# Adjacency steps of one chunk of edges instead of two, with 24 x 131 source columns, in a graph attention and expert kernel

## The chip, the cores and the metric

The kernel runs on one core of a Trainium2 chip. The time is device time in microseconds of one execution. Three runs of the kernel before took 1892.36, 1878.16 and 1903.58 us; the median is 1892.36.

## The reference, cut to what matters

There are 3125 nodes with 256 features and 100000 edges, sorted by destination. A graph attention layer, then an expert layer; both add to x.

```python
x = _layernorm(x)
q, k, v = linear(x, wq, bq), linear(x, wk, bk), linear(x, wv, bv)
scores = jnp.sum(q[dst] * k[src], axis=-1) * scale          # one per edge
scores = scores + (edge_weight[:, None] @ we + be)[:, 0]
exp_s = jnp.exp(scores - segment_max(scores, dst)[dst])
attn = exp_s / jnp.maximum(segment_sum(exp_s, dst)[dst], 1e-12)
out = segment_sum(v[src] * attn[:, None], dst)
x1 = layer_norm(x + out + linear(x, ws, bs), g1, b1)
x2 = layer_norm(x1 + linear(gelu(linear(x1, w_ff1, b_ff1)), w_ff2, b_ff2), g2, b2)
# then for each node: expert = argmax of 32 router logits, out = relu(relu(xf @ W1[e] + b1[e]) @ W2[e] + b2[e])
```

## The kernel before, in words

The kernel turns the edge list into a dense matrix and does dense attention with it: adj[d, s] is the sum, over the edges from s to d, of exp of their edge term; an attention weight is adj[d, s] x exp(q.k).

**Ahead of the steps (0 to 157 us).** VectorE works on the edges, 98 rows of 1024 (8 chunks of 128 edges each): edge terms, guards by scans, a code for each edge (destination and block of its source), and the powers of the source's place in its block. It also counts which chunk each step reads: comparisons of a row of NS = 98 x PS entries (PS = 8/SUB, so NS = 392) with the step numbers, one for each of SBLK = 8 blocks of 128 slots (L990, L991), and 5 more for the windows (L1017, L1018). The edge table then goes to HBM, GpSimd gathers the chunks of each step with SBLK x SUB = 16 indirect DMAs (L598) and sets a row of ones by a memset (L602), VectorE makes the codes relative (L1026), TensorE transposes them into tables and ScalarE copies these. TensorE and ScalarE make k, q, v and x ws of the 25 node tiles beside that.

**The steps (157 to 888 us).** Destinations are cut into 625 windows of WIN = 5 nodes, edges into chunks of 128. One step handles SUB = 2 neighbouring chunks for one window: 1015 steps, in NG = 512 groups of GROUP = 2, so a group has GC = 4 chunks. `turns` unrolls BODY = 16 groups as one turn of a hardware loop; the first and the last turn are written out. For each chunk:

- TensorE, `distances` (L1356): a small bf16 product gives for each edge and each of LO = 128 columns the squared distance between the column and the source's place in its block, less one;
- ScalarE, `columns` (L784): relu with the scale -(edge term) turns it into Ys, the edge term in one column and zero elsewhere;
- VectorE, `one_hot` (L1055): Xs, a one-hot of the edge's code (window row x 25 blocks of 125 sources), two chunks in one operation of 128 x 250;
- TensorE, `product` (L1371): Xs (as weights) times Ys, summed over the step's two chunks in PSUM, two passes each (f32).

Then VectorE, `sums` (L1081), adds for each of the group's two steps the step before times keep (0 or 1) to the product, into `stage`, and SP stores `stage` to adj (L523). A sum reads the sum before it, so it waits for it: the group's second on sum_ord, the first on sums_ready. VectorE's order is sum, one_hot, sum, one_hot; the one-hots are for three groups ahead (STAGES = 4 buffers). In the loop each sum and each one-hot has a register instruction in front of it, which works out the place in the table.

TensorE's order per group g is: wait for Ys of g, distances of g + 2, wait for Xs of g, product of g. SP loads the powers every 8 groups, and stores zeros to xs_dram every 8.

**Attention (888 to 1487 us).** 25 tiles of 125 destinations: SP's and GpSimd's gather of the 125 last adj rows (L625), scores in SCH = 7 chunks of columns (L1392; 6 x 512 and 128; six matmuls each, four PSUM banks), `exclude` (L1104) and the maximum on VectorE (L1112), exp on ScalarE (L793), times adj on VectorE (L1122), transposes (L1411) and the product with V (L1404). TensorE runs scores of t + 1 ahead of the transposes of t. The first two tiles' gathers start in the middle of the steps.

**Behind it (1487 to 1886 us).** Feed-forward, router, and the 56 expert tiles.

## Time and profile before

| | |
|---|---|
| median of three runs | 1892.36 us |
| span of the profiled execution | 1885.6 us (the page gives no other time of it) |
| TensorE busy | 1656.9 us, 88% |
| VectorE busy | 1193.9 us, 63% |
| ScalarE busy | 965.5 us, 51% |
| one-hots, L1055 | 1024 x 412 ns |
| sums, L1081 | 1023 x 344 ns |
| relus, L784 | 2048 x 369 ns |
| granted clock of TensorE, mean | 0.917 |

A time such as 344 ns is from the start of an instruction until its last result is written. The next one on the same engine can start earlier, so group times are read from starts. The granted clock is 1.00 at 2.4 GHz and 0.50 at 1.2 GHz. Idle time of an engine counts only where it sets the end.

### The profile page before, as it was taken

Reading aid. Unit: us, or ns where it says so; the run is one execution under the profiler, and the core shown is the slowest. Engines: PE = TensorE matmul, PEld = TensorE weight load, DVE = VectorE, ACT = ScalarE, POOL = GpSimd, SP = SyncE. Lnnn points to the kernel's source line nnn. Section 1 sums busy time; section 2 is a strip of 40 time slices with the busy share of each in tenths; the row PEclk is TensorE's granted clock in tenths of the full one; section 3 lists DMA queues with packets and bytes.
Section 4 is the critical chain, followed back from the end, with each engine's and each line's share of the span. In section 5 each row is a group of like instructions: output and inputs, shape, how many; then the busy total and the mean of one; then the engine's idle time right before and its main releaser. Section 6 shows DMA issues by size and latency. Waiting matters only on the chain.

```text
span 1885.6 us, 41069 instructions
## 1 busy us (share of the span) xinstructions
PE 1656.9 (88%) x11015; PEld 1378.6 (73%) x11015; DVE 1193.9 (63%) x3327; ACT 965.5 (51%) x2962; POOL 300.8 (16%) x397
## 2 busy tenths in 40 slices
PE   2898999999799999999899999999999789419960
PEld 1796888888688888887688888888888779315640
DVE  3927898988688889898555555555555578701111
ACT  1566888888588888887233333333333345103210
POOL 0022000000000000000111111111110067375435
PEclk9999999999899999999999999999999889656555
DMA  6054333333433333334822222222210100047634
GB/s 159 28 129 115 104 105 104 106 103 105 140 104 104 106 105 103 104 105 112 164 76 77 76 76 76 76 78 75 76 75 37 53 17 0 6 117 214 181 113 121
DMA packets 226999, 180.40 MB, mean 96 GB/s; under 512 B 41884, under 2 KB 218038, under 8 KB 223544
## 3 DMA queue, kind: packets, MB, share of 16 engines
q1 hardware_dynamic: 189327, 112.46, 21.6%
q0 software_dynamic: 21408, 61.20, 9.7%
q10 hardware_dynamic: 16224, 6.27, 1.5%
q8 instruction: 17, 0.28, 0.1%
q14 instruction: 23, 0.19, 0.0%
HBM read 84.94 MB, written 99.11 MB: 98 GB/s over the span
## 4 chain that ended last, share of the span: by engine, by line
PE 78%; DVE 6%; DMA 5%; POOL 4%; issue 3%; SPq 2%; ACT 1%; POOLq 0%; DVEq 0%; ACTq 0%
PE bank L1371 29%; PE bank L1404 15%; PE bank L1392 11%; PE bank L1356 9%; PE bank L1411 3%; PE bank L1486 3%; PE bank L1493 2%; PE bank L1478 2%; PE bank L1444 2%; PE bank L1436 2%; POOL arena L691 2%; POOL xs_dram L669 2%; SPq L458 1%; DMA V<-in_x 1%; DMA arena<-in_x 1%
## 5 line engine op out<-in xcount | busy, mean ns | idle before, releaser
L784 ACT ACTIVATE arena<-bank,tables 128x128 f32<-128x128 f32 x2048 | 585.2, 369 | 144.5 <-PE bank L1356 144.4
L1371 PE MATMUL bank<-arena 128*125 128x128 f32 x4096 | 585.9, 286 | 11.8 <-DVE arena L1055 11.8
L1371 PEld LDWEIGHTS bank<-arena 128*125 128x125 f32 x4096 | 488.4, 188 | 65.1 <-DVE arena L1055 11.9
L1055 DVE TENSOR_TENSOR arena<-iota_row,tables 128x250 f32<-128x250 f32 x1024 | 421.1, 412 | 0.1
L1081 DVE SCALAR_TENSOR_TENSOR arena<-arena,tables,bank 125x128 f32<-125x128 f32 x1023 | 351.9, 344 | 86.5 <-PE bank L1371 37.1
L1404 PE MATMUL bank<-V,arena 125*125 125x256 f32 x1250 | 296.4, 382 | 5.6 <-ACT arena L810 5.6
L810 ACT COPY arena<-bank 125x500 f32<-125x500 f32 (+1 forms) x175 | 90.8, 533 | 379.5 <-PE bank L1411 379.5
L1404 PEld LDWEIGHTS bank<-V,arena 125*125 125x125 f32 x1250 | 223.3, 188 | 38.0 <-ACT arena L810 10.3
L1122 DVE CUSTOM_DVE_ANT_0 arena<-arena 125x3200 f32<-125x3200 f32 x25 | 87.3, 3493 | 222.2 <-ACT arena L793 222.2
L622 POOL COPY gidx<-arow 125x1 uint32 (+1 forms) x25 | 36.4, 1455 | 1182.2 <-DVE wk_sb L1122 856.7
L1356 PE MATMUL bank<-dist_rhs,arena 5*128 5x128 bf16 x2048 | 201.6, 218 | 4.2 <-DVE tables L1039 3.4
L1356 PEld LDWEIGHTS bank<-dist_rhs,arena 5*128 5x128 bf16 x2048 | 113.8, 93 | 66.3 <-issue 4.0
L1392 PE MATMUL bank<-k_hi,q_hi 128*125 128x512 f32 (+1 forms) x350 | 137.7, 393 | 10.3 <-DVE wk_sb L1112 6.9
L1392 PE MATMUL bank<-k_lo,q_hi 128*125 128x512 f32 (+1 forms) x350 | 133.2, 380 | 0.0
L1392 PE MATMUL bank<-k_hi,q_lo 128*125 128x512 f32 (+1 forms) x350 | 133.2, 380 | 0.0
L1112 DVE CUSTOM_DVE_ANT_0 arena<-bank,arena 125x512 f32<-125x512 f32 (+1 forms) x175 | 103.0, 631 | 28.0 <-PE bank L1392 19.1
L793 ACT ACTIVATE arena<-arena,wk_sb 125x512 f32<-125x512 f32 (+1 forms) x175 | 115.8, 679 | 9.6 <-DVE wk_sb L1117 9.6
L1271 DVE TENSOR_SCALAR arena<-bank 128x256 f32<-128x256 f32 x56 | 23.7, 424 | 152.7 <-PE bank L1493 152.7
L1411 PE MATMUL bank<-ident,arena 125*125 125x125 f32 x625 | 94.5, 276 | 2.7 <-issue 2.7
L1411 PEld LDWEIGHTS bank<-ident,arena 125*125 125x125 f32 x625 | 88.7, 190 | 9.4 <-issue 3.1
L1392 PEld LDWEIGHTS bank<-k_hi,q_hi 128*125 128x125 f32 x350 | 65.9, 188 | 30.5 <-DVE wk_sb L1112 13.2
L1478 PE MATMUL bank<-ident,V 128*128 128x128 f32 x112 | 37.2, 434 | 55.1 <-DMA V<-xs_dram 55.1
(219 smaller groups left out, 1665.5 us busy)
## 6 DMA issues: line engine op xcount, KB each, us to landing
adj<-arena SPq DMA_DIRECT2D x512, 125.0 KB
xs_dram<-zeros SPq DMA_DIRECT2D x64, 112.0 KB, 3.2
V<-xs_dram SPq DMA_DIRECT2D x56, 128.0 KB, 2.3
ys_dram<-arena SPq DMA_DIRECT2D x56, 128.0 KB, 1.9
w_dram<-in_L_ffn_W SPq DMA_DIRECT2D x2, 2048.0 KB
V<-in_x SPq DMA_DIRECT2D x5, 625.0 KB
q_dram<-arena ACTq DMA_DIRECT2D x25, 125.0 KB, 2.3
wq_sb<-q_dram SPq DMA_DIRECT2D x25, 125.0 KB, 7.8
```

What stands on the lines that cost most here:

```text
L784: ins = nc.scalar.activation(Ys[:, q, k, :], bank[2 + s][:, k * LO:(k + 1) * LO], ACT.Relu, scale=nval_tab[:, bass.ds(i, 1)])
L793: ins = nc.scalar.activation(Z[0:TILE, s, c:c + n], Z[0:TILE, s, c:c + n], ACT.Exp, bias=nmax[:, s:s + 1])
L810: nc.scalar.copy(PT[0:TILE, s, j:j + n, :], bank[4 + g % 2][0:TILE, 0:n * TILE].rearrange("p (n d) -> p n d", n=n)).then_inc(pt_ready, 1)
L1055: ins = V_.tensor_tensor(Xs[:, s, cols, :], iota_row[:, 0:TILE].unsqueeze(1).to_broadcast([P, SUB, TILE]), code_tab[:, bass.ds(g * GC + k ...
L1081: ins = V_.scalar_tensor_tensor(stage[0:TILE, q, k, :], prev, keep_tab[0:TILE, bass.ds(g * GROUP + k, 1)], ps, ALU.mult, ALU.add)
L1112: V_.tensor_tensor_reduce(out=Z[0:TILE, s, c:c + n], in0=bank[b % 4][0:TILE, 0:n], in1=Z[0:TILE, s, c:c + n], scale=1.0, scalar=-BIG, op0= ...
L1122: V_.tensor_tensor_reduce(out=Z[0:TILE, s, :], in0=Z[0:TILE, s, :], in1=A_sb[0:TILE, s, :], scale=1.0, scalar=0.0, op0=ALU.mult, op1=ALU.a ...
L1356: ins = mm(bank[2 + s][:, k * LO:(k + 1) * LO], dist_rows[:, j // LOADG, c:c + CHUNK], dist_rhs[:, :], start=True, stop=True)
L1371: ins = mm(o, Xs[:, j % STAGES, k, :], Ys[:, j % STAGES, k, :], start=(k % SUB == 0), stop=(k % SUB == SUB - 1))
L1392: ins = mm(bank[b % 4][0:TILE, 0:n], q[:, s, k, :], v[:, k, j, :].rearrange("p j l -> p (j l)"), start=(i == 0), stop=(i == len(parts) - 1))
L1404: ins = mm(bank[6 + s][0:TILE, 0:D], PT[0:TILE, s, j, :], V[:, j, :], start=(j == 0), stop=(j == NT - 1))
L1411: ins = tr(bank[4 + g % 2][0:TILE, j * TILE:(j + 1) * TILE], Z[0:TILE, s, (j0 + j) * LO:(j0 + j) * LO + TILE], ident[0:TILE, 0:TILE])
```

## The change

SUB goes from 2 to 1: a step is one chunk. There are 1406 steps, NG = 704 groups with GC = 2 chunks each, 44 turns for 32, SBLK = 11, NS = 784. The sources are cut into HI = 24 blocks of LO = 131 (24 x 131 = 3144 columns), so a one-hot has WIN x HI = MW = 120 columns. One operation `one_hots` makes both one-hots of a group (128 x 240), after the group's two sums. Keys are kept without gaps as 3125 columns padded to NCOL = 7 x 448, and scores go in 7 chunks of 448. Zero stores have 84 rows for 112, and there are 88 for 64. TensorE's product has two added waits on sums_ready.

```diff
-SUB = 2
+SUB = 1
-LO = 128
-ROW = NT * LO
+HI, LO = 24, 131
+ROW = HI * LO
+MW = WIN * HI
+KB = 448
+NCOL = 7 * KB
-ZROWS = MT * P // (2 * TURNS)
+ZROWS = -(-MT * P // (2 * TURNS * 12)) * 12
-SCH = [(c, min(512, ROW - c)) for c in range(0, ROW, 512)]
+SCH = [(c, KB) for c in range(0, NCOL, KB)]
...
-            od(V_.tensor_copy(s_row, bank[0][:, 0:NS]))
+            od(V_.tensor_copy(s_row[:, 0:512], bank[0][:, 0:512]))
+            od(V_.tensor_copy(s_row[:, 512:NS], bank[1][:, 0:NS - 512]))
+            dve.sem_inc(s_copied, 1)
...
-            def one_hot(g, s, k):
-                cols = slice(k * SUB, (k + 1) * SUB)
-                ins = V_.tensor_tensor(Xs[:, s, cols, :], iota_row[:, 0:TILE].unsqueeze(1).to_broadcast([P, SUB, TILE]),
-                                       code_tab[:, bass.ds(g * GC + k * SUB, SUB)].unsqueeze(2).to_broadcast([P, SUB, TILE]),
-                                       ALU.is_equal)
-                if k == GROUP - 1:
-                    ins.then_inc(x_ready, 1)
+            def one_hots(g, s):
+                V_.tensor_tensor(Xs[:, s, :, :], iota_row[:, 0:MW].unsqueeze(1).to_broadcast([P, GC, MW]),
+                                 code_tab[:, bass.ds(g * GC, GC)].unsqueeze(2).to_broadcast([P, GC, MW]),
+                                 ALU.is_equal).then_inc(x_ready, 1)
...
-                        ins = V_.scalar_tensor_tensor(stage[0:TILE, q, k, :], prev,
-                                                      keep_tab[0:TILE, bass.ds(g * GROUP + k, 1)], ps, ALU.mult, ALU.add)
+                        ins = V_.scalar_tensor_tensor(stage[0:MW, q, k, :], prev,
+                                                      keep_tab[0:MW, bass.ds(g * GROUP + k, 1)], ps, ALU.mult, ALU.add)
                     ins.then_inc(sum_ord if k < GROUP - 1 else sums_ready, 1)
-                    if not (isinstance(i, int) and i == TURNS - 1 and j > BODY - STAGES):
-                        one_hot(g + STAGES - 1, (q - 1) % STAGES, k)
+                if not (isinstance(i, int) and i == TURNS - 1 and j > BODY - STAGES):
+                    one_hots(g + STAGES - 1, (q - 1) % STAGES)
...
             def spread():
...
+                mm(bank[0][:, 0:512], ones[0:PP, :], s_diag[:, 0:512], start=True, stop=True)
+                mm(bank[1][:, 0:NS - 512], ones[0:PP, :], s_diag[:, 512:NS], start=True, stop=True).then_inc(rows_bc, 1)
                 pe.wait_ge(diag_set, 2)
+                pe.wait_ge(s_copied, 1)
...
                 pe.wait_ge(x_ready, g + 1)
+                wait_from(pe, sums_ready, g - STAGES + 1)
+                wait_from(pe, sums_ready, g - STAGES + 1)
...
-                        ins = mm(bank[b % 4][0:TILE, 0:n], q[:, s, k, :], v[:, k, j, :].rearrange("p j l -> p (j l)"),
+                        ins = mm(bank[b % 4][0:TILE, 0:n], q[:, s, k, :], v[:, k, c:c + n],
```

The order on VectorE inside the loop of the steps, one group before. L1081 is the sum, L1055 the one-hot; ISA is the register instruction in front of each, and the square brackets say what it waits for.

```order
L1081 ISA [waits sums_ready,stored2,prod_done]
L1081 SCALAR_TENSOR_TENSOR arena<-arena,tables,bank 125x128
L1055 ISA
L1055 TENSOR_TENSOR arena<-iota_row,tables 128x250
L1081 ISA [waits sum_ord]
L1081 SCALAR_TENSOR_TENSOR arena<-arena,tables,bank 125x128
L1055 ISA
L1055 TENSOR_TENSOR arena<-iota_row,tables 128x250
```

And one group of the change, where the sum is L1084 and the one-hot L1061:

```order
L1084 ISA [waits sums_ready,stored2,prod_done]
L1084 SCALAR_TENSOR_TENSOR arena<-arena,tables,bank 120x131
L1084 ISA [waits sum_ord]
L1084 SCALAR_TENSOR_TENSOR arena<-arena,tables,bank 120x131
L1061 ISA
L1061 TENSOR_TENSOR arena<-iota_row,tables 128x240
```

The second sum has moved up to stand right behind the first, on which it waits by sum_ord, and one of the two one-hots is gone.

On TensorE, in the written-out turn, two groups before. L1356 are the distances, L1371 the products:

```order
L1356 MATMUL bank<-dist_rhs,arena 128x128 [waits y_ready]
L1356 MATMUL bank<-dist_rhs,arena 128x128 x3
L1371 MATMUL bank<-arena 125x128 [waits x_ready]
L1371 MATMUL bank<-arena 125x128 x3
L1356 MATMUL bank<-dist_rhs,arena 128x128 [waits y_ready]
```

and in the change, where they are L1361 and L1378:

```order
L1361 MATMUL bank<-dist_rhs,arena 128x131 [waits y_ready]
L1361 MATMUL bank<-dist_rhs,arena 128x131
L1378 MATMUL bank<-arena 120x131 [waits sums_ready,x_ready]
L1378 MATMUL bank<-arena 120x131
L1361 MATMUL bank<-dist_rhs,arena 128x131 [waits y_ready]
```

Each group has half the matmuls, and the first product also waits on sums_ready.

## Rows read from the trace of the kernel before

**Rows 1.** source line L1081, the sums on VectorE: durations, first and last start

```profile
L1081 DVE SCALAR_TENSOR_TENSOR arena<-arena,tables,bank x1023: 332/346/349, 162.1 to 887.7; 125x128 f32<-125x128 f32 x171
L1081 DVEq FUSED_REGOPS  x960: 65/70/90, 185.0 to 866.5; - x192
```

**Rows 2.** chain of waits, 510 to 520 us (start us, us, what)

```profile
514.88 0.33 PE bank L1356 x4
515.20 1.07 PE bank L1371 x8
```

**Rows 3.** windows A:B: length, busy (x) of PE PEld DVE ACT POOL, PEclk, DMA share, GB/s

```profile
157.00:163.50 6.50, 5.57 (x31) 4.72 (x32) 3.81 (x12) 4.36 (x16) 0.00 (x0) 0.50 0.01 3
210.00:478.00 268.00, 268.00 (x2311) 224.80 (x2309) 240.92 (x770) 219.75 (x770) 0.10 (x1) 1.00 0.37 104
478.00:501.00 23.00, 11.23 (x98) 9.36 (x96) 8.77 (x29) 10.15 (x36) 3.15 (x4) 0.79 0.55 183
```

**Rows 4.** timeline of VectorE: start us, us, instruction, count, [idle before <-releaser]

```profile
499.31 0.35 DVE L1081 SCALAR_TENSOR_TENSOR arena<-arena,tables,bank 125x128 f32<-125x128 f32 x1 [13.54 <-DMA adj<-arena]
...
511.63 0.34 DVE L1081 SCALAR_TENSOR_TENSOR arena<-arena,tables,bank 125x128 f32<-125x128 f32 x1
511.89 0.41 DVE L1055 TENSOR_TENSOR arena<-iota_row,tables 128x250 f32<-128x250 f32 x1
512.26 0.35 DVE L1081 SCALAR_TENSOR_TENSOR arena<-arena,tables,bank 125x128 f32<-125x128 f32 x1
```

**Rows 5.** timeline of VectorE in one attention tile

```profile
1036.29 0.16 DVE L1131 RECIPROCAL wk_sb<-wk_sb 125x1 f32<-125x1 f32 x1
1036.61 0.48 DVE L1133 SCALAR_TENSOR_TENSOR ws_sb<-bank,wk_sb,x 125x256 f32<-125x256 f32 x1
1037.12 0.48 DVE L1137 SCALAR_TENSOR_TENSOR ws_sb<-bv_row,wk_sb,ws_sb 125x256 f32<-125x256 f32 x1
...
1038.30 0.43 DVE L1139 BATCH_NORM_STATS2 wv_sb<-x  x1 [0.23 <-DVE x L1138]
```

**Rows 6.** page, DMA issues: KB each, median us from issue to landing

```profile
ys_dram<-arena SPq DMA_DIRECT2D x56, 128.0 KB, 1.9
```

**Rows 7.** source line L517, the zero stores

```profile
DMA to landing us min/median/max: 2.5/3.2/4.6
```

**Rows 8.** timeline of VectorE ahead of the steps

```profile
68.50 0.76 DVE L983 TENSOR_SCALAR arena<-arena 98x1024 f32<-98x1024 f32 x1
...
75.46 0.43 DVE L990 TENSOR_SCALAR arena<-arena,step_col 128x392 f32<-128x392 f32 x1
75.92 0.56 DVE L991 TENSOR_REDUCE cnt<-arena 128x1 f32<-128x392 f32 x1
```

**Rows 9.** timeline of GpSimd: the first gather, and the memset behind the last

```profile
125.43 1.16 POOL L598 DMA_INDIRECT arena<-edge_tab,cidx  x1 [107.24 <-DMA edge_tab<-arena]
...
145.49 6.91 POOL L602 MEMSET arena<- 2x8192 bf16 x1
```

**Rows 10.** timeline of TensorE's weight loads in the scores of one tile

```profile
1008.39 0.18 PEld L1392 LDWEIGHTS bank<-k_hi,q_hi 128*125 128x125 f32 x1 [0.24 <-DVE wk_sb L1112]
...
1011.05 0.18 PEld L1392 LDWEIGHTS bank<-k_hi,q_hi 128*125 128x125 f32 x1
1011.28 0.18 PEld L1392 LDWEIGHTS bank<-k_lo,q_hi 128*125 128x125 f32 x1
1011.39 0.19 PEld L1392 LDWEIGHTS bank<-k_hi,q_lo 128*125 128x125 f32 x1
```

**Rows 11.** instructions by form, 1003 to 1164 us, x count | busy us, mean ns

```profile
L793 ACT ACTIVATE arena<-arena,wk_sb 125x512 f32<-125x512 f32 x42 | 30.5, 727 | 0.0
...
L793 ACT ACTIVATE arena<-arena,wk_sb 125x128 f32<-125x128 f32 x7 | 2.7, 391 | 0.0
```

**Rows 12.** chain of waits, 159 to 165 us, at the half clock

```profile
159.54 2.00 PE bank L1371 x8
161.54 0.54 PE bank L1356 x4
```

More of the change, by code:

```diff
@@ L112, in gnn_moe @@
         ones = sb("ones", [P, P])
-        iota_row = sb("iota_row", [P, P])
+        iota_row = sb("iota_row", [P, LO])
         step_col = sb("step_col", [P, SBLK])
@@ L137, in gnn_moe @@
         row = {k: v[0] for k, v in rows.items()}
-        with nc.sbuf_tensor("kT", [P, KH, NT, LO], F32) as kT, nc.sbuf_tensor("tables", [P, KH * ROW], F32) as tables:
+        with nc.sbuf_tensor("kT", [P, KH, NCOL], F32) as kT, nc.sbuf_tensor("tables", [P, KH * NCOL], F32) as tables:
             pass
-        k_lo = sb("k_lo", [P, KH, NT, LO], F32R)
-        k_hi = sb("k_hi", [P, KH, NT, LO], F32R)
+        k_lo = sb("k_lo", [P, KH, NCOL], F32R)
+        k_hi = sb("k_hi", [P, KH, NCOL], F32R)
         q_hi, q_lo = sb("q_hi", [P, 2, KH, TILE], F32R), sb("q_lo", [P, 2, KH, TILE], F32R)
@@ L153, in gnn_moe @@
         x1 = sb("x1", [TILE, NT, D])
-        ARENA = 19050
+        ARENA = 19260
         arena = sb("arena", [P, ARENA])
@@ L176, in gnn_moe @@
         assert SBLK * SUB * TABW <= edges_only
-        cmp_o = view(4 * P)
-        s_row, o_row, iota_c = view(4 * P), view(4 * P), view(4 * P)
-        cmp_s, s_row, o_row, iota_c = (v[:, 0:NS] for v in (cmp_o, s_row, o_row, iota_c))
+        cmp_o = view(NS)
+        s_row, o_row, iota_c = view(NS), view(NS), view(NS)
+        cmp_s = cmp_o
         diag_flat = view(SBLK * P)
@@ L295, in gnn_moe @@
             "code_set", "idx_set", "rel_set", "tabT_done", "tab_set", "keep_set"))
-        gath_in = [sem(f"gath_in{b}") for b in range(SBLK)]
+        s_copied = sem("s_copied")
+        gath_in = [sem(f"gath_in{b}") for b in range(-(-SBLK // 2))]
+        gathered = [16 * min(2, SBLK - 2 * b) for b in range(-(-SBLK // 2))]
         last_set, last_stored, last_in, arow_set = (sem(n) for n in ("last_set", "last_stored", "last_in", "arow_set"))
@@ L329, in gnn_moe @@
         x_t = x.rearrange("(t p) d -> p t d", p=TILE)
-        xs_v, ys_v = (v.ap().rearrange("(j p) d -> p j d", p=P) for v in (xs_dram, ys_dram))
+        xs_v, ys_v = (v.ap()[0:MT * P, :].rearrange("(j p) d -> p j d", p=P) for v in (xs_dram, ys_dram))
         out_t = out.rearrange("(t p) d -> p t d", p=TILE)
@@ L523, in put @@
                 sp.dma_start(adj_v[:, bass.ds(g * GROUP, GROUP), :],
-                             stage[0:TILE, j % STAGES, :, :]).then_inc(stored[j % STAGES], 16)
+                             stage[0:MW, j % STAGES, :, :]).then_inc(stored[j % STAGES], 16)
             turns(sp, put)
@@ L581, in _ @@
                            allow_small_or_imprecise_dtypes=True).then_inc(consts_set, 1)
-            nc.gpsimd.memset(kT[:, :, :, TILE:LO], 0.0).then_inc(consts_set, 1)
+            nc.gpsimd.memset(kT[:, :, N:NCOL], 0.0).then_inc(consts_set, 1)
             nc.gpsimd.memset(minus_half[:, :], -0.5).then_inc(consts_set, 1)
@@ L758, in _ @@
                 act.wait_ge(tabT_done, b + 1)
-                ps = bank[6 + b % 2][:, :].rearrange("p (c u i) -> p c i u", c=2, u=SUB)
+                ps = bank[6 + b % 2][:, 0:2 * SUB * P].rearrange("p (c u i) -> p c i u", c=2, u=SUB)
                 def steps(tab):
@@ L799, in key_parts @@
                 c, n = SCH[b]
-                j = slice(c // LO, (c + n) // LO)
-                nc.scalar.copy(k_hi[:, :, j, :], kT[:, :, j, :]).then_inc(k_hi_set, 1)
+                nc.scalar.copy(k_hi[:, :, c:c + n], kT[:, :, c:c + n]).then_inc(k_hi_set, 1)
             def weights(t, s, t_next, u):
@@ L1121, in weigh @@
                 dve.wait_ge(e_ready, t + 1)
-                V_.tensor_tensor_reduce(out=Z[0:TILE, s, :], in0=Z[0:TILE, s, :], in1=A_sb[0:TILE, s, :], scale=1.0,
+                V_.tensor_tensor_reduce(out=Z[0:TILE, s, :], in0=Z[0:TILE, s, :], in1=A_sb[0:TILE, s, 0:NCOL], scale=1.0,
                                         scalar=0.0, op0=ALU.mult, op1=ALU.add, accum_out=den[:, s:s + 1]).then_inc(p_ready, 1)
@@ L1317, in spread @@
                 pe.wait_ge(diag_set, 1)
-                mm(bank[0][:, 0:NS], ones[0:PP, :], s_diag, start=True, stop=True).then_inc(rows_bc, 1)
+                mm(bank[0][:, 0:512], ones[0:PP, :], s_diag[:, 0:512], start=True, stop=True)
+                mm(bank[1][:, 0:NS - 512], ones[0:PP, :], s_diag[:, 512:NS], start=True, stop=True).then_inc(rows_bc, 1)
                 pe.wait_ge(diag_set, 2)
+                pe.wait_ge(s_copied, 1)
                 mm(bank[1][:, 0:4 * PP], ones[0:PP, :], e_diag, start=True, stop=True).then_inc(rows_bc, 1)
```

63 lines of the change are left out of this document (31 added, 32 removed).

## The prediction

> **What bounds the kernel now.** The page's list of groups puts most of the time into the adjacency steps, so I read these lines first. Their sums on VectorE run from 162.1 to 887.7 us [rows 1]: 725.6 us. In the chain of waits a group of this stage is four distance matmuls (L1356, 0.33) and eight product passes (L1371, 1.07), nothing else [rows 2]: 1.40 us, or 1.39 by the starts. The windows show TensorE busy without a gap at a granted clock of 1.00 [rows 3]. Check: 512 groups x 1.39 = 712, and one stall of 13.54 us on an adj store [rows 4] makes 725.5. That is the stage.
>
> The timeline of VectorE shows how near the next bound is. Where its product was there in time, the starts are sum, +0.26 one-hot, +0.37 next sum [rows 4], at most 0.63 for such a pair, so 1.26 of the 1.39 us. A sum lasts 0.35 us, yet an independent successor starts 0.26 after it: they overlap.
>
> **TensorE's side of the change.** Two distances and four product passes are left per group: half of 1.39, 0.70 us (131 columns for 128 add 2%, 120 loaded columns for 125 take as much off). ScalarE's relus take 219.75/770 = 0.29 us each [rows 3], 0.6 a group. Both fall under VectorE, so TensorE leaves the bound.
>
> **VectorE's side.** A group was sum, one-hot, sum, one-hot; each sum waits for the sum before it, and a one-hot lay between. Now it is sum, sum, one-hot: the second sum reads what the first wrote and waits for its end with nothing between. No sum follows a sum directly in this trace, so I bound the gap by other pairs in which VectorE waits for its own last result, in the attention loop [rows 5]: L1133 to L1137 starts 0.03 after the end; L1131 to L1133, which has an operand at an address from the loop's register, 0.16; L1138 to L1139 0.23. A sum in the loop has a register instruction of 65 to 90 ns in front of it [rows 1], and in the order of instructions the wait sits on that one, so it can't run ahead. I take 0.16, the pair with the same ingredients; the ends are 0.03 and 0.23. The group is then
>
> - first sum to second: 0.35 + 0.16 = 0.51
> - second sum to one-hot: 0.26
> - one-hot (240 elements for 250, -0.01) to the next group's sum: 0.36
>
> together 1.13 us. There are 1406 steps of one chunk, in 704 groups (1015 of two chunks, in 512, before): 704 x 1.13 = 796 us, where 712 stood.
>
> The Trainium skill, VectorE: DVE Perf Modes, section "The DRAIN you can't avoid", says that a semaphore between chained operations costs nothing extra, because the next one waits for the pipe anyway. By it the pair would cost 0.35, the group 0.97 and the stage 683. The trace speaks against it twice: an independent successor does start earlier (0.26), and L1133 starts later.
>
> **The stores.** 512 stores of 125 x 2 x 128 elements become 704 of 120 x 2 x 131, 88.5 MB for 65.5. DMA share was 0.37 [rows 3]; by bytes and time it goes to 0.37 x 1.35 x 712/796 = 0.45. Each of the four slots is written again 4 x 1.13 - 0.86 = 3.7 us after its last sum ended (0.86 is the 0.51 and 0.35 above). Landings near it: 1.9 us for ys_dram of 128 KB, and 2.5 to 4.6, median 3.2, for the zeros of the same stage [rows 6, 7]. With 0.3 us for the queue 3.2 just fits; I take no stall here. The one stall of 13.54 us, when the first two adjacency gathers run beside the stores, I keep at 8, between 0 and 14.
>
> The skill's DMA: Bandwidth & Descriptors, section on why a DMA increments its semaphore by 16, says that a transfer uses as many engines as the largest number up to 16 that divides its slowest dimension: 125 gives 5, 120 gives 15. By it the stores land sooner, and the stall goes towards 0, 8 us off the sum. A share of 0.37 with 5/16 = 0.31 inside agrees.
>
> Stage: 796 + 8 - 725.6 = **+78 us**. SP's 192 more stores and 24 more zero stores, TensorE's two added waits on sums_ready (true long before, since the one-hots of the group come after that sum) cost nothing: TensorE has 0.4 us free per group; without that cover they are under 0.1 a group.
>
> **Ahead of the steps.** NS doubles to 784 columns, SBLK goes from 8 to 11. A compare of 392 columns takes 0.43 us and a pass over 1024 0.76 [rows 8], so 784 cost 0.63; a reduction of 392 takes 0.56, of 784 about 0.97 (doubled: 1.12). With gaps a pair is 1.7 for 1.06: 11 x 1.7 - 8 x 1.06 = +10, the five window pairs +3, the second copy of s_row with TensorE's wait for it and three diag blocks +2: VectorE feeds the edge table 15 later. Against it, 11 indirect gathers stand for 16, which took from 125.43 to 145.49, 1.25 each: -6; and the memset behind them, 6.91 [rows 9], beside which VectorE's last additions crawl, halves: -3. Node work on TensorE hides beside all of it. **+6**, between 0 and +14.
>
> **Attention.** The scores go from 6 x 512 + 128 columns to 7 x 448, six matmuls a chunk. Their starts are 0.23 us apart at 512 and 0.11 at 128 [rows 10]; at 448, by the line between, 0.21. In all TensorE has 42 x 0.21 = 8.8 for 36 x 0.23 + 6 x 0.11 = 8.9. But its fifth chunk already waits 0.24 for VectorE to free a bank [rows 10], so the first four gain nothing, and the last three go from 12 x 0.23 + 6 x 0.11 = 3.4 to 18 x 0.21 = 3.8. On the path that frees the bank ScalarE's last exp grows from 0.39 to 0.67, the one before shrinks by 0.06 (both by the line through 512 and 128 columns [rows 11]), VectorE's shorter row takes 0.15 off: +0.1. So 0.3 for 23 middle tiles, **+7**, between -4 (TensorE's total alone counts) and +12. The gather's row shrinks 2% and lands with room. Behind attention nothing changes.
>
> **Sum.** 1885.6 (span of the profiled execution) + 78 + 6 + 7 = 1977. The median of the runs shown, 1892.36, lies 6.8 over the span, so 1983.
>
> **Rivals.**
> *The own wait is cheap.* If the register instruction does not hold up the second sum, the gap is 0.03 and the group 1.00: 704 + 8 - 725.6 + 13 = -1, so 1892, no change. It decides from a gap of 0.07 down. For it: L1137. Against: L1133, and where the wait stands in the order. This is the case on the other side, chance 0.12. The skill's sentence on the DRAIN is this case with a gap of 0.
>
> *TensorE's clock falls*, since it now idles 0.4 of every 1.13 us. At the stage's start, with the granted clock at 0.50 of full speed, the 1.2 GHz level [rows 3], eight passes took 2.00 and four distances 0.54 [rows 12]; half of it is 1.27 a group, over VectorE's 1.13. All the way that is 704 x 1.27 + 8 - 725.6 + 13 = +189, 2082; for a part of the stage, between. Against: the clock fell where TensorE stood still for microseconds (0.79 around the stall [rows 3]), and no row shows it beside short gaps. Chance 0.12.
>
> *A store late for its slot.* Rows of 524 bytes start off any round address. If every landing took the 4.6 us of the slowest zeros, the group would be (4.6 + 0.3 + 0.86)/4 = 1.44: 2202. Against: a share of 0.45. Chance 0.03.
>
> *VectorE overlaps the two sums as independent ones*: 0.88 a group, 620 us, 1807. Against: the wait is in the code. Chance 0.05, with all else that would be faster.
>
> **Numbers.** Forecast, chance 0.68: 1983, its own range 1945 to 2030 (a gap of 0.12 to 0.20 gives 1955 to 2011, then the ends of the two smaller terms). With the clock case the range is 1940 to 2080, which leaves out 0.2. Two per cent, about what can be told from no change, is 38 us: slower by more 0.82, within 0.13, faster 0.05.
>
> **What would show it.** In the profile of the changed kernel: the second sum 0.51 after the first, groups 1.13 apart; TensorE busy for 0.6 to 0.7 of the steps, product passes waiting for VectorE's one-hot; the first sum near 168 us; attention tiles 23.4 us apart for 23.1. I am wrong if second sums start within 0.40 of the first, if the granted clock is under 0.9 in the steps, or if VectorE waits for adj stores in many groups.

## The result, and the profile of the changed kernel

The changed kernel takes **2232.93 us** (median of 4 runs, 2224.66 to 2235.33) against 1895.07 of the kernel before on the same chip (4 runs): ratio **1.179, 95% interval [1.173, 1.185]**. The forecast was 1983, its range ended at 2080. The direction was right, the size was not: +338 us came for +91.

The groups of instructions of the changed kernel (out<-in, count | busy, mean ns of one | idle before, releaser), and its adj stores (KB each, median us to landing):

```profile
L1378 PE MATMUL bank<-arena 128*120 128x131 f32 x2816 | 863.8, 462 | 12.2 <-DVE arena L1061 12.2
L1084 DVE SCALAR_TENSOR_TENSOR arena<-arena,tables,bank 120x131 f32<-120x131 f32 x1407 | 494.3, 351 | 340.3 <-PE bank L1378 214.2
L1061 DVE TENSOR_TENSOR arena<-iota_row,tables 128x240 f32<-128x240 f32 x704 | 282.2, 401 | 0.0
adj<-arena SPq DMA_DIRECT2D x704, 122.8 KB, 2.3
```

L1084 is what L1081 was [rows 1]. The sums spend 214.2 us waiting for TensorE's product (L1378): TensorE has not left the bound.

TensorE's granted clock over the span in 40 slices (9 is 0.9 to 1.00), and two windows (columns as in [rows 3]):

```profile
PEclk9995555555555555555555899999999998965565
```

```profile
157.00:163.50 6.50, 2.86 (x10) 1.58 (x10) 6.21 (x15) 2.19 (x10) 2.51 (x1) 0.56 0.63 152
200.00:400.00 200.00, 200.00 (x809) 139.90 (x808) 137.30 (x405) 85.32 (x270) 0.00 (x0) 0.50 0.37 93
```

The kernel before also began its steps at 0.50. TensorE's first distance matmul of the steps starts at 157.1 us there, and from 163.6 us the clock is 1.00 but for a dip around the stall (0.79 from 478 to 501 us [rows 3], 0.90 in the 19 us behind it). In the changed kernel the first distance matmul starts at 165.5 us, and the clock stays at 0.50, the 1.2 GHz level, through all of its steps.

The source line of the sums (ns min/median/max, first and last start):

```profile
L1084 DVE SCALAR_TENSOR_TENSOR arena<-arena,tables,bank x1407: 350/351/354, 168.9 to 1225.2; 120x131 f32<-120x131 f32 x176
```

The steps last 1225.2 - 168.9 = 1056.3 us, for 725.6: **+330.7**. The first sum comes 168.9 - 162.1 = 6.8 later. Behind the last sum there are 997.7 us, for 997.9: -0.2. Together 337.3, which is the difference of the spans, 2222.9 - 1885.6.

The chain of waits in these steps (start us, us, what) is TensorE alone, as in [rows 2]:

```profile
500.01 0.33 PE bank L1361 x2
500.34 1.16 PE bank L1378 x4
```

A group is two distance matmuls (0.33) and four product passes (1.16): 1.49, and 704 of them are 1049 us. The next group starts at 501.50.

VectorE's timeline there:

```profile
501.83 0.35 DVE L1084 SCALAR_TENSOR_TENSOR arena<-arena,tables,bank 120x131 f32<-120x131 f32 x1 [0.51 <-PE bank L1378]
502.34 0.35 DVE L1084 SCALAR_TENSOR_TENSOR arena<-arena,tables,bank 120x131 f32<-120x131 f32 x1 [0.15 <-DVE arena L1084]
502.60 0.40 DVE L1061 TENSOR_TENSOR arena<-iota_row,tables 128x240 f32<-128x240 f32 x1
```

The second sum starts 0.51 after the first, [0.15] behind its end: that step of the forecast came as worked out. But in most groups (616 waits) VectorE then waits for TensorE's product, here 0.51.

Only the turns that are a loop have the gap of 0.15. The first and the last turn are written out; their sums have no register instruction in front and no operand at an address from a register. Two of their sums, first start to last end, take 0.74 (0.35, 0.04, 0.35), where in the loop they take 0.85:

```profile
171.50 0.74 DVE L1084 SCALAR_TENSOR_TENSOR arena<-arena,tables,bank 120x131 f32<-120x131 f32 x2 [0.43 <-PE bank L1378]
```

### The profile page after: what moved, and what is told of

It is laid out like the page before. It is cut to its first block, busy times and chain, and to the rows that moved or that the text cites. A ratio compares the mean times of both kernels' runs of the same rounds, so it can differ in the third digit from the quotient of the medians.

```text
span 2222.9 us, 38877 instructions
## 1 busy us (share of the span) xinstructions
PE 1982.5 (89%) x9089; PEld 1521.1 (68%) x9089; DVE 1281.6 (58%) x3408; ACT 823.4 (37%) x2328; POOL 292.6 (13%) x392
## 4 chain that ended last, share of the span: by engine, by line
PE 77%; DVE 7%; issue 4%; DMA 4%; POOL 3%; SPq 2%; ACT 2%; DVEq 0%; POOLq 0%; ACTq 0%
PE bank L1378 36%; PE bank L1409 11%; PE bank L1361 10%; PE bank L1397 7%; PE bank L1416 3%; PE bank L1491 2%; PE bank L1498 2%; PE bank L1449 2%; PE bank L1441 2%; PE bank L1483 1%; POOL arena L696 1%; POOL xs_dram L674 1%; DVE arena L1107 1%; SPq L463 1%; DMA V<-in_x 1%
## 5 line engine op out<-in xcount | busy, mean ns | idle before, releaser
L1378 PE MATMUL bank<-arena 128*120 128x131 f32 x2816 | 863.8, 462 | 12.2 <-DVE arena L1061 12.2
L1378 PEld LDWEIGHTS bank<-arena 128*120 128x120 f32 x2816 | 642.8, 311 | 155.2 <-issue 116.5
L1084 DVE SCALAR_TENSOR_TENSOR arena<-arena,tables,bank 120x131 f32<-120x131 f32 x1407 | 494.3, 351 | 340.3 <-PE bank L1378 214.2
L789 ACT ACTIVATE arena<-bank,tables 128x131 f32<-128x131 f32 x1408 | 444.5, 367 | 613.3 <-PE bank L1361 613.3
L1061 DVE TENSOR_TENSOR arena<-iota_row,tables 128x240 f32<-128x240 f32 x704 | 282.2, 401 | 0.0
L1361 PE MATMUL bank<-dist_rhs,arena 5*128 5x131 bf16 x1408 | 278.6, 299 | 3.4 <-DVE tables L1046 2.6
L1361 PEld LDWEIGHTS bank<-dist_rhs,arena 5*128 5x128 bf16 x1408 | 88.1, 104 | 175.9 <-ACT arena L789 144.5
L1397 PE MATMUL bank<-k_hi,q_hi 128*125 128x448 f32 x350 | 136.8, 391 | 23.9 <-DVE wk_sb L1115 20.7
L1397 PE MATMUL bank<-k_lo,q_hi 128*125 128x448 f32 x350 | 129.9, 371 | 0.0
L1397 PE MATMUL bank<-k_hi,q_lo 128*125 128x448 f32 x350 | 129.6, 370 | 0.0
L798 ACT ACTIVATE arena<-arena,wk_sb 125x448 f32<-125x448 f32 x175 | 114.4, 671 | 10.0 <-DVE wk_sb L1120 10.0
```

The costliest lines, as they stand in the source:

```text
L789: ins = nc.scalar.activation(Ys[:, q, k, :], bank[2 + s][:, k * LO:(k + 1) * LO], ACT.Relu, scale=nval_tab[:, bass.ds(i, 1)])
L798: ins = nc.scalar.activation(Z[0:TILE, s, c:c + n], Z[0:TILE, s, c:c + n], ACT.Exp, bias=nmax[:, s:s + 1])
L1061: V_.tensor_tensor(Xs[:, s, :, :], iota_row[:, 0:MW].unsqueeze(1).to_broadcast([P, GC, MW]), code_tab[:, bass.ds(g * GC, GC)].unsqueeze(2) ...
L1084: ins = V_.scalar_tensor_tensor(stage[0:MW, q, k, :], prev, keep_tab[0:MW, bass.ds(g * GROUP + k, 1)], ps, ALU.mult, ALU.add)
L1361: ins = mm(bank[2 + s][:, k * LO:(k + 1) * LO], dist_rows[:, j // LOADG, c:c + CHUNK], dist_rhs[:, :], start=True, stop=True)
L1378: ins = mm(o, Xs[:, j % STAGES, k, :], Ys[:, j % STAGES, k, :], start=(k % SUB == 0), stop=(k % SUB == SUB - 1))
```

## The experiments

All ratios are to the kernel before on the same chip. Where not said otherwise, an edit is made in the changed kernel. A "filler" is one f32 matmul into an unused bank behind a group's product passes; it shows as two passes, and nothing reads it. No experiment leaves anything of the computation out. In the edits, three dots stand for lines left out.

### Does the clock hold the time? Fillers of 128 columns

```diff
                 ins.then_inc(prod_done, 1)
+                mm(bank[6][:, 0:128], ones[:, :], ident[:, 0:128], start=True, stop=True)
```

> The changed kernel with one more f32 matmul of 128 columns per group behind the product, into a PSUM bank that nobody reads. Theory A (the granted clock): TensorE idles too much at full clock with half a group's matmuls, so the whole stage runs at 0.50; with the added work the clock goes to 1.00 early in the steps, and the group falls from 1.49 us to VectorE's 1.13 to 1.20: about 1980 to 2030 us in all, although TensorE does more. Rival B (hand-overs and waits bind, not the clock): the added work only lengthens TensorE's part, the group becomes 1.7 us, 2380 us in all.

Measured: **1967.03 us**, ratio 1.037 [1.018, 1.055]. Added work made the kernel 266 us faster. A window and the chain of waits:

```profile
200.00:400.00 200.00, 196.63 (x1438) 152.34 (x1437) 170.19 (x539) 113.47 (x360) 0.00 (x0) 1.00 0.50 124
```

```profile
499.79 0.65 PE bank L1378 x4
500.45 0.22 PE bank L1381 x2
500.67 0.22 PE bank L1361 x2
```

When the clock rose, in two windows:

```profile
170.00:174.00 4.00, 4.00 (x19) 3.04 (x17) 2.21 (x7) 1.27 (x4) 0.00 (x0) 0.52 0.25 63
174.00:178.00 4.00, 4.00 (x31) 3.22 (x30) 3.56 (x12) 2.52 (x8) 0.00 (x0) 1.00 0.37 90
```

The clock is 1.00 from 174 us on, 9 us after TensorE's first distance matmul of the steps (164.6 us), in TensorE's fifth group. The four passes take 0.65 for 1.16, and the group is 1.09 with the filler in it. Its sums run from 167.9 to 970.9, 803 us; the forecast's steps were 796 + 8 = 804. That the clock held the time is shown. What the filler does to the clock the runs show; by what rule, they don't.

Note that the chain is TensorE alone: 0.65 + 0.22 + 0.22 is 1.09 too. With the filler TensorE needs as long as VectorE, so this run by itself does not show VectorE's 1.09; a later one does (fillers at the start).

### Do TensorE's added waits matter?

```diff
-                wait_from(pe, sums_ready, g - STAGES + 1)
-                wait_from(pe, sums_ready, g - STAGES + 1)
```

> The changed kernel without the two added waits on sums_ready at TensorE's product. Theory A: nothing moves, 2233 us within 0.5%, clock 0.50 in the steps. Rival C (these waits tie TensorE to the sums of the group three before and set the 1.49 us): the group falls by 0.1 us or more, 2160 us or less.

Measured: 2215.66 us, 1.168 [1.157, 1.179], where the changed kernel had 1.179 [1.173, 1.185]; clock 0.50 in the steps. The two waits cost nothing that this can tell, as the prediction had it, and do not hold the clock down.

### Does the order sum, sum, one-hot matter?

```diff
...
                     ins.then_inc(sum_ord if k < GROUP - 1 else sums_ready, 1)
-                if not (isinstance(i, int) and i == TURNS - 1 and j > BODY - STAGES):
-                    one_hots(g + STAGES - 1, (q - 1) % STAGES)
+                    if not (isinstance(i, int) and i == TURNS - 1 and j > BODY - STAGES):
+                        one_hot(g + STAGES - 1, (q - 1) % STAGES, k)
```

> The changed kernel with one one-hot of 128 x 120 for each step, in the order sum, one-hot, sum, one-hot, instead of one for both steps behind the two sums. Theory A: TensorE at half clock sets the group, 2233 us within 1%. Rival D (the second sum's wait for the first, 0.16 us beyond its end, is what the change lost): the group falls by about 0.1 us, 2160 us.

Measured: 2222.61 us, 1.171 [1.153, 1.190]. With TensorE at 0.50 the order changes nothing. So I ran it again with the filler of 128 columns, where VectorE counts:

> The changed kernel with the filler of 128 columns and with one one-hot of 120 columns per step, in the order of the kernel before (sum, one-hot, sum, one-hot). With the clock at 1.00, VectorE sets the group. If the second sum's wait of 0.15 us for its own predecessor costs time (my step 0.35 + 0.16), an independent one-hot between the sums hides it: sum to one-hot 0.26, one-hot to sum 0.37, as the kernel before showed, 1.26 a group against 1.09 now, since the one-hots no longer share one instruction: 1967 + 704 x 0.17 = 2087. If the one-hot of 120 columns is shorter than that (0.33 less 0.07 for its smaller half) the group is 1.09 and the time 1967. I take 2000 to 2090; below 1967 would say that the order sum, sum, one-hot is what made VectorE slow.

Measured: **1971.66 us**, 1.051 [1.044, 1.057], the same as 1967 and below the 2000 to 2090 that I took. VectorE's timeline:

```profile
500.01 0.35 DVE L1087 SCALAR_TENSOR_TENSOR arena<-arena,tables,bank 120x131 f32<-120x131 f32 x1
500.27 0.28 DVE L1061 TENSOR_TENSOR arena<-iota_row,tables 128x120 f32<-128x120 f32 x1
500.50 0.35 DVE L1087 SCALAR_TENSOR_TENSOR arena<-arena,tables,bank 120x131 f32<-120x131 f32 x1
500.77 0.28 DVE L1061 TENSOR_TENSOR arena<-iota_row,tables 128x120 f32<-128x120 f32 x1
501.10 0.35 DVE L1087 SCALAR_TENSOR_TENSOR arena<-arena,tables,bank 120x131 f32<-120x131 f32 x1
```

Within a group sum to sum is 0.49 with a one-hot between, against 0.51 with nothing between: the one-hot fits into the own wait. From the second sum to the next group's first it is 0.60, and the group is 1.09 either way. So my 0.16 for the own wait was right, yet joining the one-hots gained nothing against keeping them apart. How much faster either order could be in the loop this run can't show, since TensorE with its filler takes 1.08 to 1.09 as well. In the written-out last turn, where VectorE catches up, a group takes it 0.97 with the one-hots joined (fillers of 128 columns) and 0.94 with them apart: the orders are near each other there too.

### Is it VectorE's pace that lowers the clock? The kernel before, slowed

In the kernel before, two (first kernel) or one (second) short reductions on VectorE follow each one-hot. TensorE's work stays eight passes and four distances.

```diff
+        spare = sb("spare", [P, 4])
...
                         one_hot(g + STAGES - 1, (q - 1) % STAGES, k)
+                        for r in range(2):
+                            V_.tensor_reduce(spare[:, k * 2 + r:k * 2 + r + 1], ident[:, :], AX, ALU.max)
```

> The kernel before with two reductions of 128 columns more on VectorE behind each one-hot (four per group), whose results nobody reads. They take about 0.2 us each, so VectorE needs 2.0 us per group for TensorE's 1.39. Theory A: TensorE, now idle for a third of the time, loses its clock over the stage, granted 0.50 in the steps, and the stage takes 512 x 2.0 to 2.4 us, 2200 to 2400 us in all. Without the clock's part it stays at 1.00 and 2.0 us per group: 2200 us.

> The kernel before with two short reductions a group on VectorE whose result is never read: its group becomes VectorE's, about 1.6 us for 1.39, with the same work on TensorE (eight product passes, four distances), so TensorE stands idle about 0.2 of each group. Theory A (idle pieces as such don't lower the clock; too little multiplied per time does): the clock stays at 0.95 to 1.00 in the steps, 512 x 1.6 = 820 us, 1985 to 2005 us. A rival by which any idle piece in each group lowers it: clock 0.50, a group near 2.6, 2450 or more.

Measured: 2170.17 us, 1.144 [1.122, 1.166], and 1969.22, 1.044 [1.025, 1.062]. A window of each:

```profile
200.00:400.00 200.00, 168.79 (x1231) 137.61 (x1230) 200.00 (x823) 117.80 (x412) 0.00 (x0) 0.89 0.27 75
```

```profile
200.00:400.00 200.00, 187.29 (x1538) 149.62 (x1537) 200.00 (x769) 146.40 (x514) 0.00 (x0) 1.00 0.33 93
```

The second came 16 us under its range (1985 to 2005), the first 30 us under its own (2200 to 2400). With TensorE shown busy for 187 of 200 us the clock stayed at 1.00. With 169 of 200 it was 0.89, where I had expected 0.50; it swings, as two shorter windows of that kernel show:

```profile
305.00:310.00 5.00, 4.98 (x35) 4.04 (x35) 5.00 (x22) 2.56 (x10) 0.00 (x0) 0.77 0.23 65
310.00:315.00 5.00, 3.98 (x35) 3.10 (x33) 5.00 (x22) 3.16 (x12) 0.00 (x0) 1.00 0.24 67
```

A regular idle piece is thus not enough to put TensorE at 0.50 for good: in the slowed kernel, which idles 0.48 us in each group and has eight passes in one stretch, the clock came back each time. Which part of the changed kernel's group makes the difference (four passes in a stretch, the length of the idle piece, the other shape) these two runs do not separate.

### How much filler, and where?

64 columns behind each group:

```diff
+                mm(bank[6][:, 0:64], ones[:, :], ident[:, 0:64], start=True, stop=True)
```

128 columns behind every second group:

```diff
+                for _ in range(1 if j % 2 == 0 else 0):
+                    mm(bank[6][:, 0:128], ones[:, :], ident[:, 0:128], start=True, stop=True)
```

> The changed kernel with a filler of 64 instead of 128 columns behind each group's product passes (its result is never read). Theory A (TensorE's clock stays at 0.50 because of how much it stands idle in the steps; VectorE alone would give a group of 1.09): half the filler leaves TensorE more idle, so the clock is between the two cases seen: either mostly 0.50 with the group at 1.49 plus about 0.1 (filler at half clock), 2225 to 2300 us, or partly 1.00 and the time between 1967 and 2230. I take 2050. Theory D (any additional matmul breaks the pattern, whatever its size): 1967 again.

> The changed kernel with the filler of 128 columns behind every second group: as many filler columns as in the kernel with 64 in each (2454 us, clock 0.50 throughout), in half as many instructions. If what counts is how much TensorE multiplies per time, the clock stays at 0.50 here too: groups of 1.49 and 1.49 plus about 0.3, 704 x 1.64 = 1155 us of steps, 2310 to 2340 us. If the group with the filler lifts the clock and the one without drops it, it swings: 2000 to 2250. I take 2320.

Measured: **2453.68 us**, 1.307 [1.296, 1.318], and 2378.11, 1.260 [1.248, 1.272]: the slowest of all. I missed the first by 400 us and the second, whose clock I had right, by 58. The first one's window:

```profile
200.00:300.00 100.00, 100.00 (x445) 82.13 (x444) 56.42 (x166) 34.85 (x110) 0.00 (x0) 0.50 0.31 77
```

TensorE is shown busy without a gap, and is at 0.50 throughout. "Busy" in such rows does not tell that the clock will be high. Half of the filler columns, either way, buys none of the clock and costs its full time.

### Does the clock hold by itself once it is up?

Two fillers a group in the first 16 groups alone:

```diff
+                for _ in range(2 if isinstance(i, int) and i == 0 else 0):
+                    mm(bank[6][:, 0:128], ones[:, :], ident[:, 0:128], start=True, stop=True)
```

> The changed kernel with two fillers of 128 columns a group in the first 16 of the 704 groups alone, none behind them. Theory A1 (a clock once at 1.00 stays there, since VectorE then sets a group of 1.09 with TensorE busy some two thirds of it, as it stays at 0.50 once it is there): 1970 to 2000 us, granted clock 1.00 behind the first 16 groups. Theory A2 (the steps of the changed kernel give TensorE too little to keep its clock, from whatever level they start): the clock falls back to 0.50 within some groups, 2225 us. I take A2, since the kernel with fillers of 64 columns stayed at 0.50 although TensorE was shown busy without a gap there.

Measured: 2202.46 us, 1.167 [1.156, 1.179]. The fillers' source line (its last one starts at 191.7 us), two windows, and TensorE's timeline:

```profile
L1381 PE MATMUL bank<-ident,ones x64: 270/275/421, 168.5 to 191.7; 128*128 128x128 f32 x64
```

```profile
206.00:210.00 4.00, 2.98 (x21) 1.91 (x20) 3.39 (x12) 1.90 (x6) 0.00 (x0) 1.00 0.47 114
210.00:214.00 4.00, 3.90 (x16) 2.99 (x16) 3.07 (x10) 1.89 (x6) 0.00 (x0) 0.50 0.51 130
```

```profile
205.31 0.71 PE L1378 MATMUL bank<-arena 128*120 128x131 f32 x4 [0.16 <-DVE arena L1061]
205.95 0.28 PE L1361 MATMUL bank<-dist_rhs,arena 5*128 5x131 bf16 x2
206.39 0.71 PE L1378 MATMUL bank<-arena 128*120 128x131 f32 x4 [0.16 <-DVE arena L1061]
207.04 0.28 PE L1361 MATMUL bank<-dist_rhs,arena 5*128 5x131 bf16 x2
207.74 0.71 PE L1378 MATMUL bank<-arena 128*120 128x131 f32 x4 [0.42 <-DVE arena L1061]
208.38 0.28 PE L1361 MATMUL bank<-dist_rhs,arena 5*128 5x131 bf16 x2
209.02 0.68 PE L1378 MATMUL bank<-arena 128*120 128x131 f32 x4 [0.35 <-DVE arena L1061]
```

This is the changed kernel as I had forecast it: clock 1.00, TensorE waiting [0.16] for VectorE's one-hot, groups 1.08 to 1.10 apart (205.31 to 206.39). The clock was 1.00 for 18 us without a filler: TensorE first caught up, with groups 0.86 apart, then ran ten groups at VectorE's pace. Then two groups came late (idle 0.42 and 0.35), the clock fell at 210 us, and did not come back within the steps. I took the second theory, A2, and its 2225; the fall came, though later than within some groups.

What made the first one late stands in VectorE's timeline: a sum waited for an adj store to free its slot, so the one-hot behind it and TensorE's product came late.

```profile
206.52 0.85 DVE L1084 SCALAR_TENSOR_TENSOR arena<-arena,tables,bank 120x131 f32<-120x131 f32 x2 [0.18 <-DMA adj<-arena]
```

The zero stores of xs_dram share that queue. Moving them behind the steps might clear the way, so I did that, with and without the fillers at the start.

```diff
-                if j % LOADG == 0:
-                    sp.dma_start(xs_dram.ap()[...], zeros[0:ZROWS, 0:D]).then_inc(xs_zeroed, 16)
...
             turns(sp, put)
+            with sp.Fori(0, 2 * TURNS) as i:
+                sp.dma_start(xs_dram.ap()[bass.ds(i * ZROWS, ZROWS), :], ...).then_inc(xs_zeroed, 16)
```

> The kernel with fillers in the first 16 groups alone, and the zero stores of xs_dram (88 of 84 KB, two per 16 groups) moved behind the steps, so that few adj stores come late for their slot. Theory H (VectorE-bound groups of 1.09 hold the clock at 1.00 until one disturbance; at 0.50 they never bring it back): the clock stays at 1.00 much longer than the 34 us of its partner, until the next disturbance (the adjacency gathers beside the steps at the latest): steps of 850 to 1000 us, 2010 to 2160 in all. Theory L (these groups give too little and the fall only takes its time): it falls by about 210 us again, 2200 to 2225.

> The changed kernel without fillers, the zero stores moved behind the steps. Both theories: the clock is at 0.50 from the start of the steps and stays there, 2200 to 2235 us. Anything under 2150 would mean that the zero stores, not the groups themselves, keep the clock down.

Measured: 2239.32 us, 1.194 [1.186, 1.203], and 2277.97, 1.215 [1.205, 1.225]. Both are above the times of all the theories, because of what follows the steps: from attention's first row pass to its last it is 608 us in both, for 564 in the changed kernel; the moved stores now lie beside it. A window and TensorE's timeline of the first:

```profile
208.00:216.00 8.00, 7.26 (x34) 5.19 (x34) 6.60 (x21) 3.68 (x12) 0.00 (x0) 0.66 0.43 104
```

```profile
206.84 0.68 PE L1379 MATMUL bank<-arena 128*120 128x131 f32 x4 [0.35 <-DVE arena L1062]
207.45 0.28 PE L1362 MATMUL bank<-dist_rhs,arena 5*128 5x131 bf16 x2
208.11 0.68 PE L1379 MATMUL bank<-arena 128*120 128x131 f32 x4 [0.38 <-DVE arena L1062]
```

The late groups are still there, so these stores do not make them, and the experiment does not tell its two theories apart: the clock fell between 208 and 216 us again, behind late groups again. VectorE shows a second source of them just before the fall:

```profile
209.31 0.35 DVE L1085 SCALAR_TENSOR_TENSOR arena<-arena,tables,bank 120x131 f32<-120x131 f32 x1 [0.34 <-issue]
```

That is the start of a turn of the loop. The kernel with fillers in all groups has the same delay once in each turn of 16 groups; its sums' source line counts, in us and times:

```profile
  issue: 11.9, 40
```

So VectorE is late once in 16 groups whatever the stores do. Whether undisturbed groups would hold 1.00 for good stays open.

Last, the fillers in stretches, two behind each of the first 8 of every 16 groups:

```diff
+                for _ in range(2 if j < 8 else 0):
+                    mm(bank[6][:, 0:128], ones[:, :], ident[:, 0:128], start=True, stop=True)
```

> The changed kernel with two fillers of 128 columns behind the first 8 of every 16 groups: as many filler columns as one in each group, but in stretches. Eight groups with two fillers at 0.50 last about 8 x 1.9 = 15 us, near the 17 us after which the clock rose in the partners, so it should rise within one or two turns; and at 1.00 the eight groups without fillers last 9 us, less than the 18 us over which they held it. Theory H and L both: the clock is 1.00 in most of the steps, the group near 1.09 to 1.15, 1967 to 2020 us. If it stays at 0.50: 16 groups of 1.9 and 1.49 in turn, 704 x 1.7 = 1195 us of steps, 2360.

Measured: **1994.08 us**, 1.064 [1.038, 1.089]. A window, and a stretch of TensorE's timeline without fillers in which it catches up and waits for nobody:

```profile
400.00:600.00 200.00, 191.89 (x1404) 148.25 (x1404) 167.70 (x527) 110.43 (x351) 0.00 (x0) 1.00 0.49 121
```

```profile
198.97 0.28 PE L1361 MATMUL bank<-dist_rhs,arena 5*128 5x131 bf16 x2
199.19 0.71 PE L1378 MATMUL bank<-arena 128*120 128x131 f32 x4
199.83 0.28 PE L1361 MATMUL bank<-dist_rhs,arena 5*128 5x131 bf16 x2
```

The same number of fillers as one per group, and the clock at 1.00 in nearly all of the steps (0.98 in the mean), across eight groups at a time without one. The second reading is the price of my halving: at 1.00, and not waiting, a group of the changed kernel takes TensorE 199.83 - 198.97 = 0.86 us, where I had 0.70.

### Fewer hand-overs, and 125 rows a step

Four steps per group, one-hots apart, sources as 25 blocks of 128; then the same with two fillers a group:

```diff
...
-GROUP = 2
+GROUP = 4
...
-LOADG = 8
+LOADG = 4
...
-HI, LO = 24, 131
+HI, LO = 25, 128
...
```

> The changed kernel with four steps per group for two (352 groups), destination one-hots one per step between the sums, sources as 25 blocks of 128, no filler. It has the same product passes, relus and sums, but half as many hand-overs on TensorE (distances, wait, products). Theory A with a fixed hand-over per group that doesn't halve or double with the clock: at 0.50 a group of four takes 8 x 0.21 + 4 x 0.11 + 0.45 = 2.6 us, 352 x 2.6 = 915 us for 1056, so about 2090; if the clock rises because TensorE's idle pieces change, VectorE sets 2.1 to 2.5 a group: 740 to 880 us, 1900 to 2060. Theory B (TensorE's passes simply take what they take, no hand-over): 2230, as now.

> The kernel of four steps per group with two fillers of 128 columns a group, the same TensorE work per step as in the first filler run. Theory A: the clock is 1.00 in the steps, and VectorE sets the group: four pairs of sum and one-hot. By the pairs of the kernel before (0.63 where the product was there) 2.5 a group, 880 us, 2045; by the smaller one-hots of 120 columns 2.1, 740 us, 1905. I take 1970. A clock of 0.50 with 2090 or more would speak against A.

Measured: 2046.17 us, 1.090 [1.076, 1.104], and 2056.16, 1.094 [1.087, 1.102]. The first lies at the top of my case with a risen clock (1900 to 2060), the second 86 us over my 1970, and both for a reason that I had in neither: windows of both, and from the second one of VectorE's waits (us, times, longest):

```profile
200.00:300.00 100.00, 81.53 (x491) 67.84 (x491) 81.96 (x325) 46.53 (x164) 0.00 (x0) 0.72 0.38 114
```

```profile
200.00:300.00 100.00, 83.40 (x655) 72.79 (x652) 82.44 (x328) 46.84 (x164) 0.00 (x0) 0.91 0.38 114
```

```profile
DVE arena L1086 <- DMA adj<-arena: 132.0, 268, 17.0
```

The first has no filler and the same passes per step as the changed kernel, but eight in a stretch, and its clock swings between the two levels instead of staying at 0.50. The clock differs, 0.72 and 0.91, and the time does not: VectorE waits for the adj stores. The sums of the second run from 170.6 to 1049.9, 2.50 us a group, so 256,000 bytes in 2.50: 102 GB/s. With 120 rows a step 125,760 bytes went in 1.09, 115 GB/s, without such waits. So I changed only this, in the first kernel with fillers:

```diff
-HI, LO = 24, 131
+HI, LO = 25, 128
```

> The changed kernel with the filler of 128 columns (clock 1.00, VectorE's group 1.09) and with sources as 25 blocks of 128 in place of 24 of 131: 125 rows a step for 120, 4% more bytes. Theory S (a store whose rows number 125 is spread over 5 of the DMA engines, and 5 carry what the kernels with four steps a group showed at their stores' limit, 256,000 bytes per 2.43 us = 105 GB/s; 120 rows are spread over 15): 128,000 bytes per group at 105 GB/s take 1.22 us, over VectorE's 1.09, so VectorE waits for adj stores in nearly every group: 704 x 1.22 = 857 us of steps for 803, 2020 us. Theory without it (bytes alone count): 1967 to 1975, as with 120 rows.

Measured: **2069.15 us**, 1.097 [1.086, 1.107], against 1967. A window, and from its sums' source line the idle time that adj stores ended (us, times):

```profile
200.00:400.00 200.00, 182.44 (x1294) 136.16 (x1293) 164.20 (x486) 101.09 (x323) 0.00 (x0) 1.00 0.38 114
```

```profile
  DMA adj<-arena: 53.6, 137
```

The time is 49 us over even the case with slow stores. The sums run from 169.0 to 1068.5: 1.28 us a group, 100 GB/s. For 1.8% more bytes (not the 4% of my expectation: the rows are also shorter) the store became the bound; 125 rows of 128 columns carry less per time than 120 of 131. The DMA engines' mean busy share is 0.38 here and in the two kernels above, and 0.50 with 120 rows, so the bound is not that all of them are busy. By the rule of the Trainium skill, DMA: Bandwidth & Descriptors, section on why a DMA increments its semaphore by 16, 125 rows use 5 engines and 120 use 15. The runs agree in the direction; they show the rates and the share, not the engines, and since the edit changes the number of rows and their length (512 bytes for 524) at once, they don't separate the two.

No version beat the kernel before. At a clock of 1.00 VectorE needs 1.09 a group, 704 x 1.09 = 767 us, over the 712 that stood, and with a filler in each group TensorE needs as much.

## Why the prediction was wrong, step by step

**The step that failed** is "Both fall under VectorE, so TensorE leaves the bound". It holds at a granted clock of 1.00: there a group takes TensorE 0.86 for VectorE's 1.09, and TensorE waited for VectorE in ten groups behind the fillers at the start. The clock was 0.50, TensorE's group 1.49, and TensorE stayed the bound in all of the steps. The failed part is "half of 1.39, 0.70 us", a price at full clock, carried over to a kernel whose clock it had not secured. I had this as a rival with chance 0.12, on the ground that in the trace of before the clock fell only where TensorE stood still for microseconds. That trace held no stretch with 0.16 us idle in each group of four passes, and I took the missing row as evidence against. Why the clock does not rise with such groups stays open.

**The rival was mis-sized too**: 1.27 a group, 2082, for 1.49 and 2233. I halved [rows 12]: 2.00 for eight passes and 0.54 for four distances at 0.50 gave 1.00 and 0.27; measured 1.16 and 0.33. At 1.00 likewise 0.64 and 0.22 for half of [rows 2], 0.53 and 0.17. Each run of passes carries a piece that halving the passes leaves whole; the 131 columns for 128 are an estimated 0.02 of it. With 1.49 the same sum would have given 704 x 1.485 + 8 - 725.6 + 13 = +341, 2233: so the 250 us between forecast and result are 2082 - 1983 = 99 for the clock at my halved prices and 151 for those prices. That this sum meets 2233 to the microsecond is partly luck: the waits on stores were 15 for 8, and the end was 8 us shorter.

**VectorE's group**: second sum 0.51 behind the first, as forecast; one-hot to sum 0.33 for 0.36, so 1.09 for 1.13. At 1.00 the steps took 803 for 804, in part by chance. A group of 1.09 makes 767 of the 796. What filled that up I did not have: 17.4 us of waits on adj stores for my 8, the 11.9 us at the starts of turns, and the groups at 0.50, at the beginning and in a dip behind the stall. The cheap own wait (a gap of 0.03 or 0) did not come in the loop, where [0.15] stands in front of the second sum; it came in the two written-out turns, with 0.04. So the condition of that rival was the right one: it is the register instruction and the operand that goes with it that cost 0.11 of the 0.15. The Trainium skill, VectorE: DVE Perf Modes, section "The DRAIN you can't avoid", has the semaphore between chained copies cost nothing extra. The pairs without a register instruction agree to within 0.04, those with one do not. My evidence of the early independent successor was none against the page: it lets a next operation that isn't held start earlier. What the prediction did not see is that a one-hot can lie in the own wait free, and so that sum, one-hot, sum, one-hot fits into the same 1.09.

**Stores**: landing 2.3 us, better than my 3.2; the waits on them were 15.0 us in three, for 8. A group of 1.49 hides more than one of 1.13 would; at 1.09 there were 17.4 us in four, so they held there too, with 120 rows. The DMA share at that pace was 0.50, for my 0.45.

**Ahead of the steps**: +6.8 for +6. **Attention**: its term came as well. The line of its row pass in the kernel before and in the changed one:

```profile
L1122 DVE CUSTOM_DVE_ANT_0 arena<-arena x25: 3492/3493/3494, 907.9 to 1463.9; 125x3200 f32<-125x3200 f32 x25
```

```profile
L1125 DVE CUSTOM_DVE_ANT_0 arena<-arena x25: 3425/3426/3427, 1245.7 to 1809.6; 125x3136 f32<-125x3136 f32 x25
```

From the first tile to the last 563.9 for 556.0: +7.9, forecast +7. What follows the last tile's row pass, which the change hardly touches, was 8 us shorter in this execution (413.3 for 421.7), which left -0.2 in all. That is scatter: the same stretch lasted between 391 and 426 us in the profiled executions of this document, without order in it.

## What to carry to other kernels

Before an edit takes work off TensorE, price the whole stage at a granted clock of 0.50 as well, with what each run of dependent matmuls costs whatever its length: if that time is above the new bound, the edit may give back more than it saved, and a trace in which TensorE never paused briefly cannot rule it out. If the clock does fall, a matmul that nobody reads is a cheap test and sometimes a cure, but too small a one makes it worse. When rows of a store change in number, look at the rate of the stores, not at the bytes. And a dependent pair of instructions in a hardware loop can cost more than the same pair written out: look at both places in the trace before pricing the wait.

## What the runs showed of the chip that I had not expected

- Two kernels in which TensorE is shown busy at 0.50 almost without a gap, one with and one without a filler of 64 columns, stayed there for over 1050 us. One filler of 128 columns a group brought 1.00, 9 us after TensorE's first matmul of the steps. Half as many, one in every second group, did not (0.50 throughout); as many, two in each of eight groups and none in the next eight, did.
- The Trainium skill, TensorE: Matmul & The Clock Gate, section "A second HAM failure mode: psum-queue depth-cycling", tells of short idle pieces between groups that make the clock swing between its levels. The slowed kernel before shows that swing (0.89). The changed kernel shows another thing: no swing, but 0.50 for all of the 1056 us. Once there, slower TensorE is the bound of the group, so that nothing else in the kernel makes it pause, and it still is not granted more.
- Stores of 125 rows of 128 columns stopped at 100 to 102 GB/s, stores of 120 rows of 131 ran at 115 without holding VectorE up.
- A sum that waits for the sum before it starts 0.15 us behind its end in the loop, with a register instruction in front, and 0.04 behind it in the written-out turns, without one. An independent one-hot of 0.28 us fits between two such sums of the loop for nothing (0.49 from start to start, for 0.51).
- Each turn of the loop starts VectorE's first sum about 0.3 us late (40 times, 11.9 us).
